# Ternary and rank parts of the up projection as products of their own, in a two-layer fp32 kernel on one core

## What is computed

```
q, k, v = x @ wq + bq, x @ wk + bk, x @ wv + bv          # 16 heads x 64 = 1024 columns
Q, K    = elu(q) + 1, elu(k) + 1
attn    = Q * sum(K * v) / (Q * sum(K) + eps);  out = gelu(attn @ wo + bo)
tern(w) = clip(round(w / s), -1, 1),  s = mean(|w|) of each row of w
h       = x @ (tern(w_fc) * s).T + gate * (x @ v.T @ fast_b.T @ u.T)     # 256 -> 1024, rank 16
r       = max(h, 0);  y = (r * r) @ (tern(w_proj) * s).T                 # 1024 -> 256
```

## Time and profile before

| | |
|---|---|
| median of 3 runs | 2966.96 us (2963.73 to 2968.0) |
| the profiled execution: its time, its span | 2968.17 us, 2966.4 us |
| TensorE busy, mean granted clock | 2873.0 us (97%), 0.989 |
| VectorE, ScalarE, GpSimd busy | 80%, 73%, 64% |
| attention half, layers' half (by the first instruction of the latter) | to 1798.6 us, from there to 2966.4 us |

### The profile page before, as it was taken

How to read it: one execution, slowest core, us unless ns; L and a number is a source line. 1 busy time by engine, 2 the same in 40 slices (tenths; PEclk the granted TensorE clock), 3 DMA queues, 4 the chain that set the end, 5 groups by cost and what they waited for, 6 DMA issues and landing times.

```text
span 2966.4 us, 60900 instructions
## 1 busy us (share of the span) xinstructions
PE 2873.0 (97%) x20655; PEld 2303.2 (78%) x20655; DVE 2366.3 (80%) x6881; ACT 2166.7 (73%) x5699; POOL 1896.8 (64%) x2486
## 2 busy tenths in 40 slices
PE   7999999999999999999999995999999999999996
PEld 5777777777777777777777774788888888888885
DVE  7888888888898798798798886777777777777775
ACT  6776776776676676676676673687888888888884
POOL 6876776776776676686686684245555555555455
PEclk9999999999999999999999997999999999999999
DMA  2000000000000000000000012000000000000000
GB/s 73 23 9 16 23 9 16 23 8 16 23 9 16 23 9 16 23 9 16 23 9 15 23 42 88 8 8 8 22 22 15 15 15 15 15 15 15 8 15 22
DMA packets 51234, 57.54 MB, mean 19 GB/s; under 512 B 3024, under 2 KB 48608, under 8 KB 50928
## 3 DMA queue, kind: packets, MB, share of 16 engines
q1 hardware_dynamic: 50352, 53.32, 5.6%
q10 hardware_dynamic: 576, 0.33, 0.0%
HBM read 36.86 MB, written 16.78 MB: 18 GB/s over the span
## 4 chain that ended last, share of the span: by engine, by line
PE 79%; ACT 9%; DVE 5%; issue 4%; POOL 3%; DMA 0%; SPq 0%; DVEq 0%; ACTq 0%; POOLq 0%
PE pj L304 17%; PE qk L369 10%; PE sc L340 9%; PE v_up L1332 7%; PE qk L384 6%; PE tp L359 5%; PE k L1332 4%; PE sc L359 4%; PE out L1423 3%; PE q L1332 3%; PE down L1423 3%; PE qk L315 2%; ACT b_y L96 2%; PE qk L322 2%; ACT b_ring L1515 2%
## 5 line engine op out<-in xcount | busy, mean ns | idle before, releaser
L735 POOL TENSOR_SCALAR a_ex<-a_ex,a_rc 128x384 f32<-128x384 f32 (+1 forms) x1024 | 537.6, 537 | 369.8 <-DVE a_rc L610 369.8
L493 ACT ACTIVATE a_ex<-a_ex,a_nm 128x384 f32<-128x384 f32 (+1 forms) x1024 | 576.0, 566 | 36.6 <-DVE a_nm L603 28.0
L603 DVE CUSTOM_DVE_ANT_0 a_ex<-sc,a_mask,a_rn 128x384 f32<-128x384 f32 (+1 forms) x1024 | 532.1, 543 | 8.1 <-PE sc L340 8.1
L1864 POOL TENSOR_TENSOR b_alo<-b_ring,b_ahi 128x512 fp32r<-128x512 f32 x128 | 169.5, 1324 | 414.3 <-DVE b_ring L1687 379.9
L499 ACT ACTIVATE a_pt<-tp 128x256 f32<-128x256 f32 (+1 forms) x512 | 222.7, 435 | 287.3 <-PE tp L359 287.3
L719 POOL TENSOR_TENSOR a_qr<-a_ra,a_rb 128x256 f32<-128x256 f32 x512 | 371.6, 737 | 84.6 <-DVE a_rb L585 84.4
L340 PE MATMUL sc<-a_kT,a_qT 64*64 64x256 f32 (+1 forms) x4096 | 307.6, 415 | 1.5 <-DVE a_nm L603 1.5
L369 PE MATMUL qk<-a_pt,a_v 128*64 128x384 f32 (+1 forms) x2048 | 304.5, 440 | 0.6 <-DVE a_pt L615 0.6
L615 DVE COPY a_pt<-sc 128x384 f32<-128x384 f32 (+1 forms) x400 | 203.8, 509 | 88.8 <-PE sc L359 83.2
L369 PEld LDWEIGHTS qk<-a_pt,a_v 128*64 128x64 f32 x2048 | 136.1, 137 | 143.1 <-issue 123.4
L584 DVE TENSOR_TENSOR a_ra<-pj,s_a_rot 128x256 f32<-128x256 f32 x512 | 213.3, 417 | 30.9 <-ACT s_a_sq L478 28.7
(11 more groups left out here) (279 smaller groups left out, 9187.4 us busy)
## 6 DMA issues: line engine op xcount, KB each, us to landing
s_res<-x SPq DMA_DIRECT2D x16, 512.0 KB, 3.9
y<-s_res SPq DMA_DIRECT2D x16, 512.0 KB, 2.9
s_y<-y SPq DMA_DIRECT2D x16, 512.0 KB, 3.9
a_xin<-x SPq DMA_DIRECT2D x15, 512.0 KB, 5.0
out<-b_y SPq DMA_DIRECT2D x15, 512.0 KB, 2.9
a_raw<-wqkv SPq DMA_DIRECT2D x6, 384.0 KB, 7.9
a_xin<-wqkv SPq DMA_DIRECT2D x8, 256.0 KB, 2.8
s_res<-wo SPq DMA_DIRECT2D x2, 512.0 KB, 4.4
```

The lines of the kernel that those rows point to most:

```text
L493: e.activation(ex[h][w][:, 0:width], ex[h][w][:, 0:width], ACT.Exp, bias=nm[:, w, h:h + 1], scale=-1.0, accum_out=rs[:, w, h:h + 1]).then_ ...
L603: e.tensor_tensor_reduce(out=ex[h][w][:, 0:width], in0=SC[w % 2][h][:, 0:width], in1=mem['mask'][:, off:off + width], scale=rn[:, par, 4 * ...
L735: e.tensor_scalar(row, row, 0.0, rc[:, w, h:h + 1], ALU.add, ALU.mult).then_inc(g['exn_pool'], 1)
```

## The change

The up projection's ternary part and its rank part become products of their own.

- **Ternary part.** The weights -1, 0, 1 are exact in fp32r (`f_t`), so they have no low part: two matmuls (y3 high, y3 low) for each half of the contraction. The row scale is applied later, in relu (`scale=st[:, 4, ...]`) and in the square, which now multiplies the bank by the scale and by r.
- **Rank part.** `v_st` (256 x 128) holds v transposed in four groups of 32 columns, one of them a low part; `pe_rank_rows` makes x @ v for a sample with four matmuls into K_BANK at c=0, behind q; `dve_rank_rows` turns it into `xv` with two VectorE operations (one group of rows becomes a low part), ahead of dve_q; and each chunk of the up product ends with one matmul of `u_st` (fast_b x u, times the gate, divided by the ternary scale) with `xv`. At c=0 that matmul waits for `xk_dve`.
- **Preparation.** Difference, sum, scaling, the product of v with the factor, the addition and the split are gone. `pe_rank` moves from (-1,1) to (0,0) and gets eight transposes that spread the inverse scales over D; `dve_rank_up` at (0,0) and `dve_rank_down` at (0,2) build the stationary operands. The scales move from (-2,6) to (-1,0), the biases' variants from (-1,0) to (-2,0), and the four bias DMAs go ahead of the weight DMAs on SP's queue. The w_proj DMAs wait for the second ternary half instead of the sum.
- **k of sample 0** uses Q_BANK for its odd chunks 1, 3 and 5; pe_k then waits for the chunk before the last, and ScalarE's relu of k, which shares a work row, waits for dve_k of the chunk before.
- **ScalarE's order.** relu of the up product moves ahead of the n4 rows (c=5) and the n2 rows (c=6).

```diff
--- before.py
+++ after.py
-RANK = 16
+RANK, RANK_STEP = (16, 32)
...
-    def dve_scales(e, count, n):
-        link(e, e.tensor_scalar(st[:, 1, 0:count], st[:, 0, 0:count], 1.0 / n, SCALE_FLOOR, ALU.mult, ALU.max))
+    def dve_scales(e, count, n, scale):
+        link(e, e.tensor_scalar(scale, st[:, 0, 0:count], 1.0 / n, SCALE_FLOOR, ALU.mult, ALU.max))
...
-        dve_scales(e, FC, DIM)
+        dve_scales(e, FC, DIM, st[:, 4, :])
+        e.reciprocal(st[:, 5, :], st[:, 4, :]).then_inc(w['rank_dve'], 1)
...
-        link(e, last)
-
-    def dve_fc_difference(e):
...
         last.then_inc(w['tern_dve'], 1)
-
-    def dve_rank(e):
-        e.wait_ge(w['wq_pool'], 4)
+        e.wait_ge(w['tern_dve'], h + 1)
+
+    def dve_rank_up(e):
+        e.wait_ge(i['rank'], 16 * 4)
+        raw = mem['u_raw']
         for k in range(2):
             e.wait_ge(w['bu_pe'], k + 1)
...
+            e.wait_ge(w['inv_pe'], k + 1)
+            e.tensor_copy(raw[:, k * 512:(k + 1) * 512], O[k][:, :]).then_inc(w['u_dve'], 1)
+            e.wait_ge(w['u_dve'], 2 * k + 1)
+            e.scalar_tensor_tensor(raw[:, k * 512:(k + 1) * 512], raw[:, k * 512:(k + 1) * 512],
+                mem['gate'][:, 0:1],
+                D[k][:, :], ALU.mult, ALU.mult).then_inc(w['u_dve'], 1)
+        e.wait_ge(w['u_dve'], 4)
+        e.tensor_copy(mem['u_st'][:, :], raw).then_inc(w['rank_dve'], 1)
+        e.wait_ge(w['rank_dve'], 2)
+        low = mem['u_st'][3 * RANK_STEP:P, :]
+        e.tensor_tensor(low, raw[3 * RANK_STEP:P, :], low.bitcast(F32), ALU.subtract).then_inc(w['rank_dve'], 1)
+
+    def dve_rank_down(e):
+        e.tensor_copy(flat(mem['v_st']), mem['v']).then_inc(w['rank_dve'], 1)
...
     def dve_weights(e, b, c):
-        if (b, c) == (-2, 6):
+        if (b, c) == (-2, 0):
+            dve_biases(e)
+        if (b, c) == (-1, 0):
             dve_fc_scales(e)
-        if (b, c) == (-1, 0):
-            dve_biases(e)
             dve_fc_less(e)
         if (b, c) in ((-1, 1), (-1, 2)):
             dve_fc_tern(e, c - 1)
-        if (b, c) == (-1, 3):
-            dve_fc_difference(e)
-        if (b, c) == (-1, 4):
-            dve_fc_sum(e)
-        if (b, c) == (-1, 5):
-            dve_fc_scaled(e)
-        if (b, c) == (-1, 6):
-            dve_rank(e)
-        if (b, c) in ((0, 0), (0, 1)):
-            dve_fc_rank(e, c)
-        if (b, c) in ((0, 1), (0, 2)):
-            dve_fc_low(e, c - 1)
+        if (b, c) == (0, 0):
+            dve_rank_up(e)
+        if (b, c) == (0, 2):
+            dve_rank_down(e)
...
     def pe_rank(e):
         e.wait_ge(i['rank'], 16 * 4)
         for k in range(2):
-            e.matmul(O[k][0:RANK, :], mem['fb'], mem['u_t'][:, k * 512:(k + 1) * 512], start=True,
+            e.matmul(O[k][:, :], mem['fb'], mem['u_t'][:, k * 512:(k + 1) * 512], start=True,
                 stop=True).then_inc(w['bu_pe'], 1)
...
+        e.wait_ge(w['rank_dve'], 1)
         e.wait_ge(w['tr_act'], 4)
...
         for k in range(2):
+            for t in range(4):
+                last = e.transpose(D[k][:, t * P:(t + 1) * P],
+                    st[:, 5, 4 * k + t:4 * k + t + 1].to_broadcast([P, P]), ident[:, :])
+            last.then_inc(w['inv_pe'], 1)
...
+    def k_bank(s, c):
+        return Q_BANK if s == 0 and c % 2 and c < HC - 1 else K_BANK
+
     def pe_k(e, s, c):
...
-        if due(HC * s + c):
-            e.wait_ge(g['ku_dve'], HC * s + c)
-        pe_chunk(e, 'k', K_BANK, s, c).then_inc(g['k_pe'], 1)
+        read = c - 1 if s == 0 and c < HC - 1 else HC * s + c
+        if due(read):
+            e.wait_ge(g['ku_dve'], read)
+        pe_chunk(e, 'k', k_bank(s, c), s, c).then_inc(g['k_pe'], 1)
...
+    def pe_rank_rows(e, s):
+        e.wait_ge(g['y3l_dve'], 2 * s + 2)
+        if s == 0:
+            e.wait_ge(w['rank_dve'], 7)
+        if inside(s + 2):
+            e.wait_ge(g['ku_dve'], HC * (s + 3))
+        else:
+            e.wait_ge(g['sq_dve'], FC * s)
+        parts = [(c, x) for c in range(DC) for x in y3_split(s)]
+        for k, (c, x) in enumerate(parts):
+            last = e.matmul(K_BANK[:, :], mem['v_st'][:, c, :], x[:, c, :], start=k == 0, stop=k == len(parts) - 1)
+        last.then_inc(g['xv_pe'], 1)
+
     def pe_up(e, s, c):
...
-        pe_split_product(e, up_bank(s, c), mem['fhi'], mem['flo'], *y3_split(s), c).then_inc(g['h_pe'], 1)
+        bank, parts = (up_bank(s, c), [(k, x) for k in range(DC) for x in y3_split(s)])
+        for n, (k, x) in enumerate(parts):
+            e.matmul(bank[:, :], mem['f_t'][:, k, c * P:(c + 1) * P], x[:, k, :], start=n == 0, stop=False)
+        if c == 0:
+            e.wait_ge(g['xk_dve'], s + 1)
+        e.matmul(bank[:, :], mem['u_st'][:, c * P:(c + 1) * P], mem['xv'][:, :], start=False,
+            stop=True).then_inc(g['h_pe'], 1)
...
         if inside(b):
             pe_q(e, b, c)
+        if c == 0 and inside(b - 2):
+            pe_rank_rows(e, b - 2)
...
-        e.activation(mem['r'], up_bank(s, c)[:, :], ACT.Relu).then_inc(g['r_act'], 1)
+        e.activation(mem['r'], up_bank(s, c)[:, :], ACT.Relu, scale=st[:, 4, c:c + 1]).then_inc(g['r_act'], 1)
...
+        if inside(b - 2):
+            act_relu(e, b - 2, c)
         if c == 5 and inside(b - 3) and b < B:
             n4.apply(e, b - 3, y3_rows(b - 3))
         if c == 6 and inside(b + 2):
             n2.apply(e, b + 2, y2_rows(b + 2), range(2) if b + 2 == 0 else range(TT))
-        if inside(b - 2):
-            act_relu(e, b - 2, c)
...
+    def dve_rank_rows(e, s):
+        e.wait_ge(g['xv_pe'], s + 1)
+        e.tensor_scalar(mem['xv'][:, :], K_BANK[:, :], mem['low_rows'][:, 0:1], None,
+            ALU.mult).then_inc(g['xs_dve'],
+            1)
+        e.wait_ge(g['xs_dve'], s + 1)
+        e.tensor_tensor(mem['xv'][:, :], K_BANK[:, :], mem['xv'][:, :].bitcast(F32),
+            ALU.subtract).then_inc(g['xk_dve'],
+            1)
+
...
-        e.scalar_tensor_tensor(mem['sq'][c % 2], up_bank(s, c)[:, :], 0.0, mem['r'], ALU.max,
-            ALU.mult).then_inc(g['sq_dve'], 1)
+        e.scalar_tensor_tensor(mem['sq'][c % 2], up_bank(s, c)[:, :], st[:, 4, c:c + 1], mem['r'],
+            ALU.mult, ALU.mult).then_inc(g['sq_dve'], 1)
...
+        if c == 0 and inside(b - 2):
+            dve_rank_rows(e, b - 2)
         if inside(b):
             dve_q(e, b, c)
```

More of the change, by code:

```diff
@@ L1100, in dve_fc_tern @@
                 fc_less[h][:, c, :], ALU.is_gt, ALU.subtract)
-        link(e, last)
-    def dve_fc_difference(e):
-        for h in range(2):
-            last = e.tensor_tensor(fc_less[h], fc_tern[h], fc_rows[h], ALU.subtract)
-        link(e, last)
-    def dve_fc_sum(e):
-        for h in range(2):
-            last = e.tensor_tensor(fc_less[h], fc_less[h], fc_rows[h], ALU.add)
-        last.then_inc(w['sum_dve'], 1)
-        e.wait_ge(w['sum_dve'], 1)
-    def dve_fc_scaled(e):
-        for c in range(FC):
-            last = e.tensor_scalar(fc_tern[c // 4][:, c % 4, :], fc_less[c // 4][:, c % 4, :], st[:, 1, c:c + 1],
-                None, ALU.mult)
@@ L1135, in dve_fc_low @@
-    def dve_fc_low(e, c):
-        for k in range(2):
-            cols = slice(k * 512, (k + 1) * 512)
-            e.wait_ge(w['fhi_act'], 2 * c + k + 1)
-            last = e.tensor_tensor(mem['flo'][:, c, cols], fc_t[c][:, cols], mem['fhi'][:, c, cols].bitcast(F32),
-                ALU.subtract)
-        if c == DC - 1:
-            last.then_inc(w['ready_dve'], 1)
+            e.wait_ge(w['inv_pe'], k + 1)
+            e.tensor_copy(raw[:, k * 512:(k + 1) * 512], O[k][:, :]).then_inc(w['u_dve'], 1)
@@ L1239, in pe_weights @@
     def pe_weights(e, b, c):
-        if (b, c) == (-1, 1):
-            pe_rank(e)
         if (b, c) in ((-1, 6), (-1, 7)):
@@ L1244, in pe_weights @@
                 pe_fc_transpose(e, n)
-        if (b, c) in ((0, 0), (0, 1)):
-            pe_fc_rank(e, c)
+        if (b, c) == (0, 0):
+            pe_rank(e)
         if (b, c) in ((0, 6), (0, 7)):
@@ L1932, in run_sync @@
         proj_tiles = io['w_proj'].rearrange('(c p) n -> c p n', p=P)
+        for dst, src in ((mem['bq'][:, :], io['bq']), (mem['bk'][:, :], io['bk']), (mem['bv'][:, :], io['bv']),
+            (mem['bo'][:, :], broadcast_rows(io['bo'], DIM))):
+            e.dma_start(dst, src).then_inc(i['bias'], 16)
         for h in range(2):
@@ L2108, in chunk_columns, with in_rank_places @@
     return np.ascontiguousarray(w.transpose(2, 0, 1, 3).reshape(P, 3 * DC, HD))
+def in_rank_places(w):
+    out = np.zeros((w.shape[0], P), np.float32)
+    for k in range(P // RANK_STEP):
+        out[:, k * RANK_STEP:k * RANK_STEP + RANK] = w
+    return out
 def chunk_bias(v):
```

87 lines of the change are left out of this document (37 added, 50 removed).

## The result

The changed kernel takes 2979.4 us (median of 6 runs, 2979.1 to 2981.9), against 2965.5 for the kernel before on the same chip: ratio 1.0047, 95% interval 1.0037 to 1.0057. That is 14 us slower, inside the range of 2947 to 2980, by half a microsecond, but above the 2970 that I named: slower by more than 0.2%, a case to which I gave 0.30. The profiled execution's span went from 2966.4 to 2980.1, +13.7 us.

A forecast was written before the change was run, and what follows sets the result against it. It took TensorE as the bound in steady samples, VectorE busiest in the set-up, a chain of waits at the end. Loop +9.5, set-up -8, end +1.5 made +3, forecast 2970 against the median 2966.96, range 2947 to 2980.

The forecast's parts named there:

- A: Rival, 40%: the steady loop lengthens to 67.95 us and cancels the set-up's gain; 2970, own range 2963 to 2977.
- D: Rival, 17%: rank build in (0,0) on the path if sample 1's k starts under 3 us earlier; 2976 to 2980.
- Steady loop: Steady samples: relu waits, VectorE's pair and what queues behind it lengthen the loop by 0.85 us; eleven loops, +9.5 us.
- The 0.36 us given for c=5: Steady stage, c=5: cost of relu ahead of the rows, about offset by earlier k of c=4 and 5; taken as 0.
- TensorE itself: +0.93 - 0.23, less about 0.3 that it had idled for y2lo, so k of c=1 is 0.64 late in all: Steady stage, c=0 to 1: rank rows added, up product shortened, idle time absorbed; k of c=1 0.64 us late.
- Four matmuls and the out product cover the pair: Up product at c=0: its last matmul, waiting for VectorE's pair, is not late, being covered by 2.4 us of work.
- Set-up: Set-up stage: less VectorE weight work and no k bank wait, chunk 7 5.4 us earlier; sum -8, ends -4 and -11.
- priced at 0.7: Set-up: k and v products from 1864.21 ran at half-clock time; 2.4 us may go, 0.7 counted.
- The end: Last steps: (16,0) +2.1 on TensorE, about +1.5 staying; (17,0) +1.8; seven shorter products -1.6; +1.5, ends 0 and +4.
- Sample 13's steps: End stage, b=15: predicted even, no change in time.
- B: Rival, 25%: TensorE stays the bound, 13 x -0.93 - 8 + 1.5 = -18.6 us, 2948; loop 66.2.
- C: Rival, 18%: relu waits don't reach q's exp, only VectorE's 1.36 us counts; loop 66.9, 2958.

The follow-up runs named there:

- experiment 1: Changed kernel with ScalarE's relu behind the LayerNorm rows of c=5 and c=6 again: 2968.2 us, ratio 1.0004.
- experiment 3: Changed kernel with VectorE's two rank operations done for sample 0 only, the other samples' low-rank rows stale: 2969.8 us, ratio 1.0013.
- 4: Changed kernel with relu and square taking constants instead of the scale column, the scales left out: 2976.2 us, ratio 1.0031.
- experiment 5: Changed kernel with relu behind the rows, VectorE's pair for sample 0 only, and relu and square with constants: 2952.7 us, ratio 0.9955.
- experiment 2: Kernel before the change with only relu moved ahead of the LayerNorm rows: 2982.9 us, ratio 1.0058.

## Why the prediction was right, and where its size was off

- **As a whole**: the likeliest case, A, named the mechanism, and its own range of 2963 to 2977 ends 2 us short of the time. The full range holds the time only because its upper end, 2980, was D's, and D's mechanism did not occur; that part is luck. Of the 10.7 us by which the traces' sum (+13.7) passes mine (+3), the end has 6.4, the loop 3.3 and the set-up 0.9.
- **Steady loop: the mechanism holds, the term was mis-sized** (+0.85 given, +1.12 measured, over 12 samples instead of 11: 12.8 us for 9.5). Rival A's marks are there: relu waits in c=5 and 6, the y3 transposes behind the read of q (0.8 us a sample instead of 1.4, since TensorE has already waited 0.4 for the read of v in the same step; the slot of c=7 is longer by 1.3 us), v behind square, the pair at 0.74 + 0.69. Experiments 1, 3 and 4 each remove one part, 5 shows that there is no other. The 0.36 us given for c=5 does not come out of the rows, which give 2086.3 + 0.04 - 2085.46 = 0.88; the 0 that went into the sum was right all the same, as the rhi behind those rows starts 25.50 us after the k instead of 25.40. The step that failed is "TensorE itself: +0.93 - 0.23, less about 0.3 that it had idled for y2lo, so k of c=1 is 0.64 late in all". It is 1.06 late (51.37 after the k of c=3, before 50.31): the idle time of 0.3 is not given back, because the second y2lo is itself behind the pair and k of c=1 needs it (without the pair, in experiment 3, the slot of c=0 falls by 0.3). I had listed y2lo among what is queued behind the pair and then asked only who waits for square. Against that, the 0.2 us of v in c=2 did not come (slot 8.17 instead of 8.40), and c=1 has +0.30 for the +0.22 of the prediction.
- **The pointer operands** (the scale columns of relu and square) were not in the account at all; taking them out gives 0.21 us of the loop and some 3 us of the time.
- **The pair's price.** I took 0.68 for each; the first costs 0.74, one hundredth under the upper bound of 0.75, the second 0.69. The Trainium skill ("VectorE: DVE Perf Modes", section "Why PSUM operands drop a tier") keeps an fp32 tensor_scalar from PSUM at the base rate; the row of 0.74 agrees, where the one on SBUF takes 0.43.
- **"Four matmuls and the out product cover the pair"** was right in the steady stage, where the list has no wait for the pair, and not in the last sample, which has no out product at that place (0.65 us at 2947.74).
- **Set-up**: -7.1 for -8, with chunk 7 and the chain within 0.3 us in this pair of traces, and the first k of chunk 1 of sample 1 7.9 us nearer for 8. But the sum is near for a reason that I had priced at 0.7. Busy times as in the earlier trace rows from the first k of sample 0 to the first of sample 3, in the kernel before, experiment 2 (which has its set-up), the changed kernel and experiment 1 (which has the changed one):

```profile
1817.00:1979.00 162.00, 145.85 (x703) 113.67 (x703) 132.44 (x300) 109.48 (x172) 59.78 (x44) 0.93 0.05 17
1817.00:1977.00 160.00, 143.18 (x702) 111.92 (x702) 131.81 (x298) 109.25 (x171) 58.67 (x44) 0.95 0.05 17
1818.00:1972.00 154.00, 139.12 (x705) 111.71 (x705) 124.23 (x290) 106.75 (x167) 57.81 (x44) 0.96 0.05 18
1820.00:1976.00 156.00, 140.71 (x705) 112.56 (x705) 124.84 (x291) 106.96 (x167) 57.73 (x44) 0.95 0.06 18
```

  At the same grant of 0.95 the stretch takes 160.3 us with the old set-up and 156.1 with the new: -4.2. The other 2.9 of the 7.1 go with the clock of the two profiled executions (chunk 7 is only 3.9 us earlier against experiment 2). Whether the change itself raises the grant there these traces can't tell. In the -4.2 there is a loss of 1.2 in the last of the three samples (56.6 us for 55.4), which has the rank rows and the pair of sample 0 and which I had put at zero; without it the work and the waits bring 5.4 where I gave 7.3. So -7.1 beside -8 is partly luck.
- **Rival D**: its condition, the first k of sample 1 less than 3 us earlier, did not occur, though the time came out at D's figure: that k starts at 1860.52 instead of 1864.21, 3.7 us (4.2 against the first k, for the 5 predicted). VectorE's chain does hold the read of k, which starts at 1865.03 right behind it where the exp was out at 1864.28, but TensorE has no gap there.
- **The end: the step failed** (+7.9 for +1.5; its own terms, 1.5 + 1.8 - 1.6, give 1.7). Sample 13's steps, "even", cost 3.0: 1.26 in the first, where rank rows and pair are added (6.42 for 5.16 us), and 1.30 in the last (6.57 for 5.27), which is the clock, as the section below shows; (16,0) cost 3.9 instead of the 2.1, since the out product, pushed behind a wait, runs at the half clock, 1.1 us dearer; from the first up product of sample 14 to that of sample 15 it took 36.5 us for 35.6, +0.9; and the seven shorter products of the last sample, priced at -1.6, gave nothing back (34.09 us for 33.97 before). Without the pair (experiment 3) that last part is 33.1, without the columns 33.7, without both 32.7: the shorter products do give 1.3, but the pair, which nothing covers there, takes 1.0 and the columns 0.4. I had counted what TensorE does in a stage that I had myself called a chain of waits. The clock's share in it differs from execution to execution (next section), so that of the 7.9 only the parts that an experiment moves are shown; the others are read from one pair of traces.
- **Rivals.** B (TensorE stays the bound, 2948) is what the change would have been with the relu left in place, a free pair and no scale columns: 2952.7 in experiment 5. C put the pair alone into the loop, 66.9; experiment 1, which is that case with the columns beside it, gives 67.22.

## What to carry to other kernels

When an operation is put into an engine's queue, ask of every instruction behind it who waits for it, and price each; the one that I followed (square) was not the only one. A change that shortens the busiest engine's work by 1% can be lost to a single operation that is moved in front of an unfinished product; look for the slack of the next loop first (0.46 us here), then move. And a stage in which every engine waits is counted along its chain, where operand forms and the clock after a pause weigh, not by what the busiest engine saves.
